# A graph-attention layer on one core: the first row group's units in another order on five engines

## The reference

```
h  = relu(layernorm(x))
Wh = h @ W
f1, f2 = Wh @ a[:128], Wh @ a[128:]
e  = leaky_relu(f1[:, None] + f2[None, :], 0.2)
e  = where(adj == 0, -inf, e)
out = x + softmax(e, axis=1) @ Wh
```

## Time and profile before

| | |
|---|---|
| median of 3 runs | 832.47 us (832.06 to 833.55) |
| profiled execution, its own time | 834.32 us |
| its span | 832.6 us |
| PE, DVE busy | 95%, 91% of the span |
| ACT, POOL busy | 59%, 49% |
| DMA queue of GpSimd | 38400 packets, 67.13 MB |

### The profile page before, as it was taken

One profiled execution on the slowest core, in us unless ns is written; L12 is line 12 of the kernel. 1 busy time (PEld: TensorE's weight loads), 2 busy tenths in 40 slices (PEclk: granted clock), 3 DMA queues, 4 the chain that ended last, 5 costly groups with the idle time before them and its releaser, 6 DMA issues.

```text
span 832.6 us, 22633 instructions
## 1 busy us (share of the span) xinstructions
PE 790.5 (95%) x8969; PEld 723.0 (87%) x8969; DVE 756.0 (91%) x1243; ACT 487.7 (59%) x793; POOL 411.7 (49%) x606
## 2 busy tenths in 40 slices
PE   3588989999999999999999999999999999999997
PEld 2477879999999999999999999999999999999986
DVE  4699999999999999999999999999999999999996
ACT  4476975555565555555565655555565656555542
POOL 4665656554554446544554446544654446543510
PEclk9899999999999999999999999999999999999999
DMA  9997579999999999999999999999999999998200
GB/s 221 117 108 73 50 76 101 106 87 100 99 87 100 89 102 90 103 86 98 98 89 101 89 103 89 102 86 97 99 88 101 87 107 88 102 88 87 26 15 17
DMA packets 43713, 75.99 MB, mean 91 GB/s; under 512 B 4768, under 2 KB 7456, under 8 KB 43680
## 3 DMA queue, kind: packets, MB, share of 16 engines
q0 software_dynamic: 38400, 67.13, 87.0%
q1 hardware_dynamic: 4864, 8.39, 3.1%
q10 hardware_dynamic: 416, 0.07, 0.0%
HBM read 272.70 MB, written 4.19 MB: 333 GB/s over the span
## 4 chain that ended last, share of the span: by engine, by line
PE 85%; DVE 7%; DMA 4%; ACT 2%; issue 1%; POOL 1%; ACTq 0%; DVEq 0%; POOLq 0%
PE acc L380 51%; PE acc L384 26%; PE stage L369 6%; DVE wt_ring L797 4%; DMA masks<-in_adj_dram 4%; DVE pairs L787 1%; DVE packed L779 1%; PE stage L360 1%; PE stage L352 1%; DVE stats L732 0%; ACT masks L564 0%; ACT marks L546 0%; ACT wh L524 0%; ACT pairs L601 0%; DVE packed L778 0%
## 5 line engine op out<-in xcount | busy, mean ns | idle before, releaser
L797 DVE SCALAR_TENSOR_TENSOR wt_ring<-stage,packed,marks 128x512 f32<-128x512 f32 x1024 | 697.6, 744 | 48.5 <-PE acc L384 42.7
L380 PE MATMUL acc<-pairs,wt_ring 128*128 128x258 f16 x4096 | 721.0, 274 | 8.1 <-DVE pairs L787 7.1
L384 PE MATMUL acc<-pairs,wt_ring 128*128 128x129 f16 x4096 | 699.3, 219 | 0.0
L380 PEld LDWEIGHTS acc<-pairs,wt_ring 128*128 128x128 f16 x4096 | 396.7, 97 | 64.0 <-issue 5.3
L546 ACT ACTIVATE marks<-stage 128x1024 uint16<-128x1024 uint8 x256 | 261.9, 1023 | 294.2 <-PE stage L369 293.3
L384 PEld LDWEIGHTS acc<-pairs,wt_ring 128*128 128x128 f16 x4096 | 400.2, 98 | 2.6
L197 POOL DMA_DIRECT2D masks<-in_adj_dram x252 | 137.8, 549 | 330.5 <-PE stage L369 307.5
L219 POOL TENSOR_TENSOR masks<-masks 128x256 int32<-128x256 int32 x256 | 179.5, 737 | 15.4 <-ACT masks L564 14.6
L564 ACT ACTIVATE masks<-masks 128x512 uint16<-128x512 uint16 x252 | 156.3, 622 | 8.5 <-DMA masks<-in_adj_dram 8.5
L369 PE MATMUL stage<-ident,masks 128*128 128x128 f32 x512 | 99.6, 276 | 2.6 <-ACT fin L637 2.0
L369 PEld LDWEIGHTS stage<-ident,masks 128*128 128x128 f32 x512 | 54.2, 142 | 6.5 <-ACT fin L637 2.3
(11 more groups left out here) (63 smaller groups left out, 160.6 us busy)
## 6 DMA issues: line engine op xcount, KB each, us to landing
masks<-in_adj_dram POOLq DMA_DIRECT2D x256, 256.0 KB, 7.1
out_dram<-xm SPq DMA_DIRECT2D x15, 256.0 KB, 7.6
xm<-in_x_dram SPq DMA_DIRECT2D x3, 1024.0 KB, 15.5
xm<-in_x_dram SPq DMA_DIRECT2D x1, 768.0 KB, 6.3
xm<-in_x_dram SPq DMA_DIRECT2D x1, 256.0 KB, 3.0
out_dram<-xm SPq DMA_DIRECT2D x4, 64.0 KB, 2.6
wx<-in_L_gnn_W_dram ACTq DMA_DIRECT2D x1, 64.0 KB, 3.2
a_sb<-in_L_gnn_a_dram ACTq DMA_DIRECT2D x1, 1.0 KB, 6.1
```

Source lines behind the costliest of these rows:

```text
L380: return nc.tensor.matmul(acc[:, r, 0:2 * E1], wtv[:, w, r, 1, :], pairv[:, t, :, 0:E1], start=st, stop=end)
L384: return nc.tensor.matmul(acc[:, r, 0:E1], wtv[:, w, r, 0, :], pairv[:, t, 0, 0:E1], start=False, stop=False)
L797: nc.vector.scalar_tensor_tensor(out=wtq[:, t % NW], in0=e_row, scalar=packed[:, t, 1:2], in1=edges[:, k], op0=ALU.max, op1=ALU.mult).then ...
```

## The change

All of it is in the first row group, but for `AHEAD`, which sets in every row group how many units ahead ScalarE multiplies the upper bytes. In words:

- The whole of row group 0's adjacency now comes in 16 parts of one unit (512 columns, four rows) instead of 4 parts and 12 loads. Ten are issued at once, six later (`EARLY`, `PARTS`). `FIRSTS` and `HALVES` say in which iteration the loads for row group 1 are issued.
- SyncE issues the last three of x's DMAs only when parts 0, 1 and 3 of the adjacency have landed; x's batches are cut as 1, 3, 2, 4 and 6 groups instead of 1, 3, 4, 4 and 4.
- The exponentials of f1 and f2 that `pack` reads lie in the free columns of PSUM bank 3 of `stage`, no longer in SBUF. So `features(g, 0)`, which writes that bank, waits for the `pack` before.
- GpSimd mixes first, then scales, then normalises, two units ahead; it normalises three of four blocks of groups 4 to 15 and ScalarE one (two and two before). VectorE normalises groups 1 and 2 whole.
- ScalarE unpacks unit b + 2 right behind the exponentials of group b + 2.
- TensorE goes through a unit tile by tile (k outside, r inside) instead of bank by bank, and has features ahead of the adjacency's transposes. W's transpose and a's product go to `stage`, the second half of group 0's features to `acc`.
- VectorE does `low_part` right behind `weights`, `inverses` of the first batch no longer behind a's product, and the statistics by a table.

```diff
-    AHEAD = 8
+    AHEAD = 6
+    EARLY = 10
-    BATCHES = [(0, 1), (1, 4), (4, 8), (8, 12), (12, 16)]
+    BATCHES = [(0, 1), (1, 4), (4, 6), (6, 10), (10, 16)]
+    STATS = {0: (6, 7), 1: (8, 9), 2: (10,), 3: (11, 12), 4: (13, 14), 5: (15,)}
...
+        exps = stage[:, 3, 256 - 2 * PACK:256].rearrange("p (r e) -> p r e", e=2)
...
-            for k in range(len(BATCHES)):
+            load_x(0)
+            load_x(1)
+            for k, part in ((2, 0), (3, 1), (4, 3)):
+                sp.wait_ge(first_loaded[part], 16)
                 load_x(k)
...
+            for u in range(EARLY):
+                load_part(u)
...
             def normalise(g):
-                for r in range(HALF, PACK):
+                for r in range(1, PACK):
...
-            for u in range(KC):
-                second(u)
-                mix(u)
-                if u == 2:
-                    scaled(1)
-                if u + 1 < NC:
-                    load_rows(u + 1)
-            load_second(NC)
+            second(0)
+            mix(0)
+            second(1)
+            scaled(0)
+            mix(1)
+            load_part(EARLY)
+            load_part(EARLY + 1)
+            scaled(1)
             for b in range(UN):
-                if b % KC == 2:
-                    load_first(NC + b // KC)
-                if 1 <= b < NQ - 1:
-                    scaled(b + 1)
+                for u in MIXES.get(b, (b + 2,)):
+                    mix(u)
+                if b + 2 < NQ:
+                    scaled(b + 2)
                 if b + 4 < NQ:
                     normalise(b + 4)
-                mix(b + KC)
-                if b % KC == KC - 1:
-                    load_second(NC + 1 + b // KC)
+                for u in PARTS.get(b, ()):
+                    load_part(u)
+                if b in FIRSTS:
+                    load_first(FIRSTS[b])
+                if b in HALVES:
+                    load_second(HALVES[b])
...
             def features(g, h, bank=None):
                 if h == 0:
                     pe.wait_ge(s["ht_ready"], g + 1)
+                    if g:
+                        pe.wait_ge(s["packed_ready"], g)
...
             for b in range(UN):
-                if b + 3 < NQ:
-                    x_transposes(b + 3)
-                pe.wait_ge(s["weighted"], b * PACK + PACK)
                 pe.wait_ge(s["pair_ready"], b + 1)
-                for r in range(PACK):
-                    products(b, r)
-                    if b + 2 < NQ and r == 0:
+                for k in range(PACK):
+                    pe.wait_ge(s["weighted"], b * PACK + k + 1)
+                    for r in range(PACK):
+                        product(b, r, k)
+                    if b + 2 < NQ and k == 0:
                         features(b + 2, 0)
-                    if b + 2 < NQ and r == 2:
+                    if b + 3 < NQ and k == 1:
+                        x_transposes(b + 3)
+                    if b + 2 < NQ and k == 1:
                         features(b + 2, 1)
-                    if r == 2:
+                    if k == 2:
                         pe.wait_ge(s["marked"], b + 2)
                         transposes((b + 2) % UN, b + 2)
```

More of the change, by code:

```diff
@@ L621, in _ @@
             relu(0)
+            keep(0, 0)
             root(1)
[L623 to L624 removed]
+            keep(0, 1, bank=0)
+            exponentials(0)
+            unpack(0, 0, first=True)
+            high_part(0)
             relu(1)
[L626 to L630 removed]
             keep(1, 0)
[L632 to L633 removed]
             keep(1, 1)
             exponentials(1)
+            unpack(1, 1, first=True)
+            relu(2)
             normalise(3)
[L637 to L638 removed]
             for b in range(UN):
[L640 to L646 removed]
                 if b + 1 < NQ:
@@ L650, in _ @@
                     keep(b + 2, 0)
-                if b == 0:
-                    root(2)
-                if b + 4 < NQ:
-                    normalise(b + 4)
+                for u in SECONDS.get(b, (b + 3,)):
+                    second(u // UN, u % UN)
+                if b in ROOTS:
+                    root(ROOTS[b])
                 if b + 2 < NQ:
@@ L808, in first_weights @@
                     dve.wait_ge(s["used"], b - 1)
-                weights(1, b)
+                weights(1, b, range(0, HALF if b == 0 else PACK))
+                low_part(b)
+                if b == 0:
+                    weights(1, b, range(HALF, PACK))
             def next_group(q):
@@ L833, in _ @@
             nc.vector.tensor_copy(e_next[:], packed[:, 0:PACK, 0]).then_inc(s["e_ready"], 1)
-            low_part(0)
+            normalise(2)
             first_weights(0)
+            pack(1)
             normalise(3)
```

201 lines of the change are left out of this document (98 added, 103 removed).

## The result

The changed kernel takes **817.31 us** (median of four runs, 816.80 to 818.83) against 832.26 us for the kernel before on the same chip; the ratio is 0.9821, with a 95% interval of 0.9804 to 0.9838. The forecast was 817.2 us.

The account below looks back on a forecast made before the run. TensorE's products bound the 15 later row groups, so only the first could gain: unit 15 due at 29.0 + 41.5 + 31.7 = 102.2 against 117.47, 15.3 us off; 834.32 - 15.3 = 819.0, less 1.85 gives 817.2 us, range 810 to 826.

Parts of the forecast that it names:

- The sum: First row group: unit 15 due (end of its `low_part`) at 102.2 against 117.47, so 15.3 us off the profiled 834.32.
- The steady stage: Later row groups: `AHEAD` at 6 asks for loads up to 5.8 us later, but TensorE stays full; 0 gained.
- Up to unit 1: Start of first row group: adjacency parts land sooner, unit 1 due at 29.0 instead of 38.75; 9.7 us off.
- The early seven: Units 1 to 8, VectorE-bound: from 78.7 us for 14 units before, less blocked time and waits, plus statistics; 41.5 us.
- The rule on the operand: VectorE's `pack`: with an operand in PSUM, L803 and L804 escape GpSimd's lock; L812, two in SBUF, stays exposed.
- The 0.61 us a unit: Blocked time of `pack`'s L779 on VectorE, taken as freed by a PSUM operand: 14 x 0.61 = 8.6 us.
- The late units: Units 8 to 15: five iterations at 4.65 by GpSimd's ring, 23.3 us, and the last two at 4.2, 8.4 us.
- ring through GpSimd: Late units: exponentials, `scaled`, three blocks of `normalise`, x's transposes, features, `keep`, next `scaled`; 4.65 us a unit.
- The lock only moves: Rival: GpSimd now blocks `low_part` instead, shown by L812 above 1 us on average; 7 us, 824; chance 0.15.
- Ten issues hold the queue up: Rival at the start: first packet waits for the last of ten issues, about 4 us later; 821; chance 0.08.
- TensorE's clock falls: Rival in the first row group: clock stays low, five units lose the gain, seven give 840 us; chance 0.04.
- It doesn't do what it says: Rival for `pack`: lock holds for PSUM operands too, features' new wait hinders; 10 us fewer, 827; chance 0.06.

Follow-up runs that it names:

- g4_ahead_8: The change with `AHEAD` back at 8 instead of 6, and two more `second` at the end of the first row group: 819.54 us, ratio 0.9833.
- g3_x_at_once: The change without the wait holding x's later DMAs behind the adjacency's parts, so all five are issued at once: 822.98 us, ratio 0.9877.
- k3_row_loads: The change with only units 0 to 3 fetched in parts, units 4 to 15 by the old row loads issued up front: 819.48 us, ratio 0.9837.
- h0_change: The change run a second time without edits, with its own profile, as reference for the other runs: 817.56 us, ratio 0.9811.
- g1: The change with the exponentials that `pack` reads in an SBUF tile instead of PSUM, order and waits untouched: 821.25 us, ratio 0.9859.
- g2: The kernel before, with only the exponentials moved to PSUM and features waiting for the `pack` before: 827.67 us, ratio 0.9936.
- h1_relu_first: The change with ScalarE's `relu` of group b + 3 ahead of the unpacking of unit b + 2: 816.77 us, ratio 0.9798.
- k2_unpack_late: The change with ScalarE unpacking the next unit at the start of its iteration instead of right behind the exponentials: 820.28 us, ratio 0.9837.

## Why the prediction was right

**The sum: 15.3 us forecast off the profiled time.** Measured in the first profile: unit 15 due at 101.75 where 102.2 was forecast, 15.7 us off. Three terms add up to that with errors that partly cancel: unit 1 0.2 us too high, the early seven 1.4 too high, the late seven 1.1 too low. That the median came within 0.1 us is luck; two profiles of the same kernel differ by 2.4 us in span, and part of the difference from before (TensorE's clock at its lower level for 13.6 us there, 6.8 in the first profile of the change) may be the clock's. The parts, in the prediction's order:

*The steady stage, 0.* Right for the step (46.92 us). GpSimd did fall back behind ScalarE: the largest wait of the changed profile that isn't ScalarE's for TensorE is GpSimd's for `second` (14.6 us in all before), and none of it reaches TensorE.

```profile
POOL masks L242 <- ACT masks L602: 240.1, 120, 2.6
```

But `AHEAD` is not worth nothing. I argued only from the supply of bytes; in g4_ahead_8 the step to the first spread is 1.0 us longer, 0.6 of it by the two `second` that stand ahead of the emptying of `acc`. In the sum it didn't show: the step from unit 15 to the first spread was 13.04 against 13.11 before, so the other edits to the transition use up what `AHEAD` gives. I didn't take those apart.

*Up to unit 1, 9.7 us.* Measured 9.95 (38.75 to 28.80; forecast 29.0). The steps hold: part 0 at 10.0 as forecast, and no wait of ScalarE for the adjacency. g3_x_at_once puts 5.3 us of it on the order of x alone; k3_row_loads shows that what the later parts are worth, 2.5 us, comes only behind unit 1.

*The early seven, 41.5 us.* Measured 40.1 in the first profile and 38.3 in the one with a clock of 1.00, so the term was too high by 3.2 us where the clock doesn't fall. The failed step is the start from 78.7 us, out of which I took only the waits that are in the earlier trace rows. These windows are the kernel before from unit 1 to 15, and then the change (h0_change) in its early and its late seven units:

```profile
38.75:117.47 78.72, 67.34 (x646) 59.51 (x645) 72.86 (x150) 64.32 (x145) 47.60 (x71) 0.95 0.78 75
```

```profile
28.82:67.08 38.26, 31.88 (x317) 27.70 (x318) 37.47 (x113) 28.45 (x65) 28.50 (x45) 1.00 1.16 119
67.08:99.92 32.84, 30.80 (x318) 27.36 (x316) 26.50 (x50) 28.55 (x61) 24.05 (x39) 1.00 0.65 64
```

VectorE was busy 72.86 us before, so it sat idle 5.9 us and not the 3.9 that I took away: 2.0 us of other gaps stayed in as if they were work, and in the early seven only 0.8 us of idle time is left (38.26 - 37.47). The work should then be 72.86 - 8.6 - 1.8 + 2.6 = 65.1; it was 37.47 + 26.50 = 64.0, and the late seven hold 0.6 more of it than the 25.9 that I gave them. Idle time 1.2, work 1.1, the split 0.6 and the 0.4 that I added for `low_part` make the 3.2 us. The sizes of `pack` (10.4 us freed; 15.2 - 4.7 = 10.5 measured) and of the 12 statistics (40 in the early seven where before had 28 in all, at some 0.21 us each) were right. In the early seven VectorE is full, 37.47 of 38.26, as the forecast had it. That the first profile shows 40.1 is TensorE's clock, at 0.91 over the stretch.

*The rule on the operand.* The 0.61 us a unit was taken from the row of L797, and g1 and g2 show it on `pack` itself, in both orders. The Trainium skill (SBUF — State Buffer, "SBUF: two separate sides") says that a lock is taken by a VectorE instruction with two inputs in SBUF, against a GpSimd instruction that reads SBUF, or in a two-port mode. The trace agrees for L804 beside `scaled` (0.91 or 0.17 us) and for L812, which has both inputs in SBUF and still goes to 1.0 or 1.4 us when it meets GpSimd. It doesn't agree for L804 beside `normalise`, where g1 shows 0.18 to 0.22. L803 has one input in SBUF and was blocked as well (three times in 14, 1.01 to 1.03 us; 351 ns on average with `exps` in SBUF, 166 in PSUM); no run shows in which mode it works.

*The late units, 23.3 + 8.4 us.* Measured 23.96 for five (4.77 the middle one) and 8.88 for two. The size was near and **the bound was another one**. My ring through GpSimd was put together rightly, and h1_relu_first shows it at 4.54 to 4.63 us, but it comes second. The step that failed is ScalarE's. I had costed it by its busy time alone, 3.6 us a unit (it was 4.1, 20.45 us in five units), and so I missed that its unpacking stands between the exponentials and `relu`, in a ring with TensorE of 4.77. That this is only 0.12 us from the ring that I had forecast is luck: the two share some steps, but nothing makes them equally long. A busy share doesn't show such a ring; the chain of waits of the changed kernel does in ten lines.

*The rivals.* "The lock only moves": in small part in the change (means of 768 and 829 ns, where 690 is free and the sign was 1000), and more in k2_unpack_late. "Ten issues hold the queue up": no; the queue moved 99 packets in 7 to 7.5 us and 417 in 8 to 10, GpSimd issuing until 9.42. Its first packet came in 5.5 to 6 us, and in 7 to 7.5 with ten issues but x asked for at once (g3_x_at_once), as in the kernel before. So x ahead of it held it, and not the issues. "TensorE's clock falls": it does, for 3.4 us at a time, and costs about 0.9 us for each fall, two in one profile of the change and none in the other. It never stayed low. "It doesn't do what it says": the operand's part was smaller than I had it in the end. `pack` fell by 10.5 us, of which undoing the operand brings back 6.5, and 2.9 to 4.0 us of time; in the old order it is worth 5.0 us. The rest of the 10.5 comes with the new order: `pack` was held by `scaled` 10 times in the 14 units before and 8 times in g1_exps_sbuf, and no longer behind DMA issues as well. The freed VectorE then waits for others.

**Where the 15 us are.** Undone one at a time: x behind the parts 5.5 us (4.7 by the ratio in the first result), the operand in PSUM 3 to 4, the unpacking behind the exponentials 2.9, parts instead of row loads for twelve units 2.1, tile order 0. These make some 14 of the 15 us, but they needn't add up, and the features' place ahead of the adjacency's transposes and VectorE's new order at the start were not tried alone.

## What to carry to other kernels

Put a tiny operand where its reader meets no lock, and then ask at once which instruction will stand under the lock instead. When an engine that was full gets free, walk every ring through the other engines in issue order, and count everything that stands between two steps of the ring on one engine (here the unpacking), since the first ring and the second may be 0.2 us apart and taking one away gives only the difference. An engine that the chain of waits names isn't the bound if its own timeline shows it standing. Subtract from an engine's busy time and from its idle time separately.

## What the runs showed of the hardware

- TensorE's granted clock fell to 0.50 for 3.4 us at a time in the first 60 us, twice in one profile of the change and not once in another of the same kernel, with unit 1 due within 0.02 us in both. Ahead of the first, from 20.0 to 29.7 us, TensorE was busy 6.00 us in the profile with falls and 6.25 in the one without, both at 1.00, which doesn't tell why one fell. Each fall cost about 0.9 us, not the 1.7 that half speed for 3.4 us would cost a full engine; TensorE was busy 33.43 of 40.10 us there. The two sets of runs of the change have medians 0.25 us apart but profiles 2.4 us apart in span, so single profiles of this kernel shouldn't be compared closer than 2 us without looking at the clock.
- A VectorE instruction on eight numbers a partition took 170 ns with its first operand in PSUM and up to 911 ns with it in SBUF, beginning under the same GpSimd instruction (`scaled`, 1.05 us) in both. In SBUF it took no more than 0.22 us beside GpSimd's `normalise`. In the kernel before it took 1.59, 1.60 and 1.62 us in three places (47.13, 93.17, 112.46), where it began while GpSimd was issuing two DMAs and ended with the `scaled` behind them.
- The time from VectorE's last instruction to the end of the span was between 3.9 and 4.4 us in thirteen profiles and 5.7 in one, for the same four output DMAs.
